# Graph attention over 32 graphs: TensorE turns every third head, the values of all groups run one graph later

## The reference

```python
q, k, v = (split_heads(x @ W + b) for W, b in ((Wq, bq), (Wk, bk), (Wv, bv)))
scores = einsum('bhqd,bhkd->bhqk', q, k) / sqrt(32) + beta * adj
scores = where(adj > 0, scores, -9e15)
out = einsum('bhqk,bhkd->bhqd', softmax(scores), v)     # heads joined again
y = layernorm(x + out)                                  # over the 384 features
```

## Time and profile before

| | |
|---|---|
| median of 3 runs | 704.23 us (703.93 to 704.75) |
| the profiled execution's own time | 703.96 us |
| its span, first to last instruction | 702.1 us |
| busy PE / DVE / ACT / POOL | 634.2 / 602.2 / 586.2 / 408.1 us |
| mean granted TensorE clock | 0.993 |
| share of the span: PE / PEld / DVE / ACT | 90% / 73% / 86% / 83% |

### The profile page before, as it was taken

The page is one execution under the profiler, slowest core; times in us unless marked ns, Lnnn a source line. Parts: engine busy times, 40 slices in busy tenths (PEclk is TensorE's granted clock), DMA queues, the critical chain, the costliest instruction groups (busy, mean ns, idle before and its releaser), DMA issues. The chain is left out here.

```text
span 702.1 us, 21340 instructions
## 1 busy us (share of the span) xinstructions
PE 634.2 (90%) x6304; PEld 514.6 (73%) x6304; DVE 602.2 (86%) x2385; ACT 586.2 (83%) x2024; POOL 408.1 (58%) x642
## 2 busy tenths in 40 slices
PE   5889999999999999999999999999999999999991
PEld 5777777777777787877787877777777777777760
DVE  3888898889898888889888989888989888989885
ACT  4798888888888889888888888888888888888891
POOL 3311466765566775556675556676556676555643
PEclk9999999999999999999999999999999999999997
DMA  7065555557655557655556755556765555765441
GB/s 247 2 159 121 135 152 139 140 139 181 171 139 153 144 122 180 174 148 151 143 123 171 181 150 152 143 126 157 181 159 144 151 137 137 181 159 127 119 104 68
DMA packets 68226, 101.93 MB, mean 145 GB/s; under 512 B 10512, under 2 KB 36368, under 8 KB 68112
## 3 DMA queue, kind: packets, MB, share of 16 engines
q1 hardware_dynamic: 67024, 100.37, 55.9%
q10 hardware_dynamic: 1088, 0.20, 0.1%
HBM read 22.94 MB, written 12.58 MB: 51 GB/s over the span
## 5 line engine op out<-in xcount | busy, mean ns | idle before, releaser
L433 ACT ACTIVATE probs<-neg_scores,neg_max 128x256 f32<-128x256 f32 x768 | 381.6, 502 | 4.6 <-DVE neg_max L515 3.1
L515 DVE CUSTOM_DVE_ANT_0 neg_scores<-s_bank,bias_sb 128x256 f32<-128x256 f32 x768 | 287.4, 414 | 62.4 <-ACT probs L433 30.8
L554 DVE STREAM_TRANSPOSE blocks<-probs 128x512 f32<-128x512 f32 x248 | 175.1, 706 | 0.0
L433 ACT ACTIVATION_READ_ACCUMULATOR probs<-neg_scores,neg_max 128x1 f32 x768 | 148.0, 193 | 0.0
L399 PE MATMUL s_bank<-qk 32*128 32x256 f32 x1536 | 110.0, 399 | 23.5 <-DVE neg_max L515 21.9
L399 PEld LDWEIGHTS s_bank<-qk 32*128 32x128 f32 x1536 | 71.2, 184 | 64.5 <-issue 48.2
L326 PE MATMUL j_bank<-xt_high,w_high 128*128 128x256 f32 x576 | 115.6, 309 | 2.0 <-ACT w_high L465 1.7
L750 POOL TENSOR_SCALAR o_sb<-y_sb,rstd,shift 128x384 f32<-128x384 f32 x60 | 98.9, 1654 | 9.6 <-POOL shift L745 9.6
L369 PE MATMUL j_bank<-ident,probs 128*128 128x128 f32 x544 | 84.2, 278 | 21.2 <-ACT xt_high L454 20.8
L326 PE MATMUL j_bank<-xt_high,w_low 128*128 128x256 f32 x576 | 99.5, 281 | 0.0
L326 PE MATMUL j_bank<-xt_low,w_high 128*128 128x256 f32 x576 | 99.5, 281 | 0.0
(11 more groups left out here) (56 smaller groups left out, 957.5 us busy)
## 6 DMA issues: line engine op xcount, KB each, us to landing
shuffled<-blocks SPq DMA_DIRECT2D x496, 128.0 KB, 2.4
x_sb<-in_x_dram SPq DMA_DIRECT2D x32, 384.0 KB, 3.3
out_dram<-o_sb SPq DMA_DIRECT2D x30, 384.0 KB, 4.3
adj_sb<-in_adj_dram SPq DMA_DIRECT2D x32, 256.0 KB, 3.8
out_dram<-o_sb SPq DMA_DIRECT2D x4, 192.0 KB, 2.1
blocks<-in_L_gnn_Wq_dram SPq DMA_DIRECT2D x1, 576.0 KB, 5.9
blocks<-in_L_gnn_Wk_dram SPq DMA_DIRECT2D x1, 576.0 KB, 8.8
blocks<-in_L_gnn_Wv_dram SPq DMA_DIRECT2D x1, 576.0 KB, 9.6
```

Of the source, the lines that this page charges most:

```text
L433: nc.scalar.activation(probs[:, (T * s + t) % (T * NX), :], neg_scores[:, (T * s + t) % (T * NH), :], ACT.Exp, bias=neg_max[:, n % 2, t, h ...
L515: nc.vector.tensor_tensor_reduce(neg_scores[:, (T * s + t) % (T * NH), :], s_bank[h % J][:, t * N:(t + 1) * N], bias_sb[:, n % 2, t, :], - ...
L554: nc.vector.transpose(blocks[:, n % 2, :, h, :, :].rearrange("p k t q -> p t k q"), probs[:, slot:slot + T, :].rearrange("p t (k q) -> p t ...
```

## The change

`by_blocks` becomes true for heads with h % 3 != 2: PE turns heads 2, 5, 8 and 11, DVE and the transfers the other eight. So each group has both kinds (3, 3 and 2 heads by DVE). O and G of group 2 move from graph n-1 to n-2 at the same steps. X of the first third moves from step 5 to step 1, K of group 1 from step 5 to 3, V of the first tile from step 3 to 5. The DVE program is put in another order within a step, with the statistics moved from step 8 to step 10 and the seed from 9 to 11. SP issues the adjacency load and the store before the load of x, and the store is that of graph n-3. POOL adds the residual after it has prepared that of the next graph. In the last graph, the copies of heads 0 to 7 go into `shuffled` (`place_of`).

```diff
     def by_blocks(n, h):
-        return n < B - 1 and h < HV
+        return n < B - 1 and h % 3 != 2
...
-                1: (("K", 0, n + 1),),
+                1: (("X", 0, n + 2), ("K", 0, n + 1)),
                 2: (("G", 1, n - 2), ("Q", 0, n + 1)),
-                3: (("V", 0, n + 1),),
-                4: (("O", 2, n - 1),),
-                5: (("X", 0, n + 2), ("K", 1, n + 1)),
-                6: (("G", 2, n - 1), ("Q", 1, n + 1)),
+                3: (("K", 1, n + 1),),
+                4: (("O", 2, n - 2),),
+                5: (("V", 0, n + 1),),
+                6: (("G", 2, n - 2), ("Q", 1, n + 1)),
...
-    last_jobs = (("G", 1, B - 1), ("O", 2, B - 1), ("G", 2, B - 1))
+    last_jobs = (("G", 2, B - 2), ("G", 1, B - 1), ("O", 2, B - 1), ("G", 2, B - 1))
...
+        def place_of(n, h):
+            if n == B - 1 and h < HV:
+                half = shuffled[:, n % 2, :, :, :, :, :].rearrange("p k a h t q -> p (k a h t q)")
+                return (half[:, h * T * N:(h + 1) * T * N].rearrange("p (k q) -> p k q", k=T), ("O", 2, n - 2))
+            i = J * n + (h // 3 if n < B - 1 else h - HV)
+            before = i - NP
+            return (probs_t[:, i % NP, :, :], ("O", (3 * (before % J) + 2) // J, before // J) if before >= 0 else None)
...
                 for k in range(T):
                     for j in range(J):
                         h = J * g + j
                         if by_blocks(n, h):
-                            probs_k = shuffled[:, n % 2, k, :, h, :, :]
+                            probs_k = shuffled[:, n % 2, k, :, h - h // 3, :, :]
                         else:
-                            probs_k = probs_t[:, turned_before[H * n + h] % NP, k, :]
+                            probs_k = place_of(n, h)[0][:, k, :]
...
-                    if h % J in (1, 2) and s + 3 < B * H:
-                        maxima(s + 3)
+                    if h % J == 1:
+                        for ahead in (s + 3, s + 4):
+                            if ahead < B * H:
+                                maxima(ahead)
+                        for job in jobs_of(n, h):
+                            take(job)
+                    elif h % J == 2:
+                        for job in jobs_of(n, h):
+                            if job[0] in "TG":
+                                take(job)
+                    if h % J in (2, 3) and s + 4 < B * H:
+                        maxima(s + 4)
                     if by_blocks(n, h):
                         turn_blocks(n, h)
-                    if h % J in (2, 3) and s + 4 < B * H:
-                        maxima(s + 4)
...
-                    if h == 8 and n >= 2:
+                    if h == 10 and n >= 2:
                         for t in range(T):
                             moments(n - 2, t)
                         gather_moments(n - 2)
-                    if h == 9 and n >= 2:
+                    if h == 11 and n >= 2:
                         seed(n - 2)
```

More of the change, by code:

```diff
@@ L76, in jobs_of @@
                 0: (("O", 1, n - 2),),
-                1: (("O", 2, n - 1),),
+                1: (("O", 2, n - 2),),
                 2: (("G", 1, n - 2),),
-                3: (("G", 2, n - 1),),
+                3: (("G", 2, n - 2),),
                 5: (("O", 0, n),),
@@ L84, in jobs_of @@
                 10: (("G", 0, n - 1), ("G", 1, n - 1)),
-                11: (("O", 1, n),),
+                11: (("O", 2, n - 1), ("O", 1, n)),
             }
@@ L234, in wait_job @@
             eng.wait_ge(job_ready, place[job] + 1)
-        def reader(i):
-            n, h = (i // J, HV + i % J) if i < J * (B - 1) else (B - 1, i - J * (B - 1))
-            return "O", h // J, n
+        def place_of(n, h):
[5 more added lines that the diff above has]
+            return (probs_t[:, i % NP, :, :], ("O", (3 * (before % J) + 2) // J, before // J) if before >= 0 else None)
         def wait_probs_free(eng, s):
@@ L270, in shuffle @@
                 if n >= 2:
-                    wait_job(sp, ("O", 1, n - 2))
+                    wait_job(sp, ("O", 2, n - 2))
                 for c in range(J):
@@ L292, in _ @@
                 shuffle(n)
+                if n + 3 < B:
+                    load_adj(n + 3)
+                if n >= 3:
+                    store(n - 3)
                 if n + 4 < B:
                     load_x(n + 4)
[L295 to L298, removed]
+            store(B - 4)
             store(B - 3)
@@ L338, in values @@
             def values(g, n, b):
-                if by_blocks(n, J * g):
+                if n < B - 1:
                     pe.wait_ge(shuffled_in[n % 2], (n // 2 + 1) * J * J * DMA)
-                else:
-                    wait_taken(pe, place["T", J * g + J - 1, n])
+                wait_taken(pe, max(place["T", h, n] for h in range(J * g, J * (g + 1)) if not by_blocks(n, h)))
                 wait(pe, taken_a, act_taken[place["V", T - 1, n] + 1])
@@ L348, in values @@
                         if by_blocks(n, h):
[L349 removed]
+                            probs_k = shuffled[:, n % 2, k, :, h - h // 3, :, :]
                         else:
[L351 removed]
+                            probs_k = place_of(n, h)[0][:, k, :]
+                            if n < B - 1:
+                                probs_k = probs_k.rearrange("p (t a q) -> p a t q", t=T, a=J)
                         mm = pe.matmul(b[HD * j:HD * (j + 1), 0:N], v_sb[:, n % 3, k, h * HD:(h + 1) * HD],
@@ L443, in take @@
                 if kind == "T":
[L444 to L447, removed]
+                    copy, left = place_of(n, a)
+                    if left:
+                        wait_job(act, left)
+                    ins = nc.scalar.activation(copy, b[:, :].rearrange("p (k q) -> p k q", k=T),
                                                ACT.Identity)
@@ L456, in take @@
                     heads, values = heads_t[:, heads_slot[a, n], :], b[:, 0:N]
-                    if by_blocks(n, J * a):
+                    if n < B - 1:
                         heads = heads.rearrange("p (t a q) -> p a t q", t=T, a=J)
@@ L526, in take @@
                     wait_job(dve, job)
[L527 to L530, removed]
+                    copy, left = place_of(n, a)
+                    if left:
+                        wait_job(dve, left)
+                    ins = nc.vector.tensor_copy(copy, b[:, :].rearrange("p (k q) -> p k q", k=T))
                 elif kind == "K":
@@ L553, in turn_blocks @@
                 slot = T * (H * n + h) % (T * NX)
-                nc.vector.transpose(blocks[:, n % 2, :, h, :, :].rearrange("p k t q -> p t k q"),
+                nc.vector.transpose(blocks[:, n % 2, :, h - h // 3, :, :].rearrange("p k t q -> p t k q"),
                                     probs[:, slot:slot + T, :].rearrange("p t (k q) -> p t k q", q=HD)).then_inc(blocks_ready, 1)
@@ L600, in norm_last @@
                     if i == 1:
-                        for job in last_jobs[1:]:
+                        for job in last_jobs[2:]:
                             take(job)
@@ L679, in _ @@
                         gather_moments(n - 2)
-                    if h == 9 and n >= 2:
+                    if h == 11 and n >= 2:
                         seed(n - 2)
-                    for job in jobs_of(n, h):
-                        take(job)
+                    if h % J != 1:
+                        for job in jobs_of(n, h):
+                            if h % J != 2 or job[0] not in "TG":
+                                take(job)
             invert(B - 1, G - 1)
-            take(last_jobs[0])
+            for job in last_jobs[:2]:
+                take(job)
             norm_last()
@@ L762, in _ @@
                 if n >= 2:
+                    add_residual(n - 2)
                     layer_norm(n - 2)
```

2 lines of the change are left out of this document (removed).

## The result

The changed kernel takes 752.06 us (median of 4 runs, 750.89 to 753.79) against 704.35 for the kernel before: 1.0679 of its time, 95% interval 1.0656 to 1.0703. I had predicted slower, 726.7 with a range of 713 to 741. The direction was right, the time lies 11 us above the range. Of the values (O and G), only those of group 2 stand one graph later than before; groups 0 and 1 keep their places, which the title puts too broadly.

What follows compares the result with a forecast made beforehand. The prediction took PE to set stretches A and B and DVE to set C, 21.65 us per graph against 20.90. The sum was 703.96 - 2.1 + 21.0 + 0.4 + 3.4 = 726.7 us, range 713 to 741.

Steps and rivals of the forecast that it cites:

- Against a rule: Two PE idles, 0.61 and 0.70, become one of 2.0 per graph; the sum nevertheless stands at the full clock level.
- Clock falls: Rival: a third of B runs at the lower clock level, 2.4 us more per graph, 790 us; chance 0.02.
- B: Stretch from step 4's to step 8's scores: PE sets it, its 0.70 wait goes, 7.40 to 7.35 us.
- A: Stretch from step 0's to step 4's scores: its 0.61 wait goes, 6.86 to 6.49 us.
- C: Stretch from step 8's scores to the next step 0: DVE sets it, PE idles 2.0, 6.64 to 7.81 us.
- The wait for X's bank: In A, PE's Q waits 0.20 us for the bank that DVE frees by taking X.
- The way in: The first two graphs, before the steady part: 37.5 us against 40.47, plus 0.9 start-up lateness, so -2.1.
- Shuffle late: Rival: the shuffle lands 2.0 us later, so PE waits 0.7 before O of group 0: +20, 746 us; chance 0.06.
- The way out: The last graphs: +0.4 us in all for graph 30 and +3.4 for the end, bounds 1.0 to 5.3.
- the last copy waits for the store of graph 29: Graph 31: that store lands at 701.4, the last copy into the same slot could begin by 698.1; 3.4 us in all.
- The copies' wait for O of group 2: Graph 31: copies of heads 0 and 1 wait for graph 29's O; ACT's chain loses about 0.8 us.
- Sum: Per graph 6.49 + 7.35 + 7.81 = 21.65 us against 20.90, +0.75; +21.0 over 28 graphs.

Runs made afterwards that it cites:

- experiment 1: Changed kernel plus 12 filler matmuls on PE in its wait ahead of the step-0 scores, graphs 2 to 29: 731.89 us, ratio 1.0396.
- experiment 3: Kernel before the change, with the statistics moved to step 10 and done twice there, second results unused: 792.88 us, ratio 1.1254.
- Experiments 4: Kernel before the change, with only the statistics moved to step 10 and the seed to step 11: 725.13 us, ratio 1.0295.
- experiment 5: Changed kernel with statistics back at step 8, seed at step 9, and POOL adding the residual first: 698.71 us, ratio 0.9922.
- experiment 7: Kernel of experiment 5, with DVE taking X and K between step 1's two maxima and step 10's block transpose first: 687.45 us, ratio 0.9762.
- experiment 9: Kernel of experiment 7, with O of group 2 of graph 29 run in the last graph's step 0, ahead of O of group 1: 686.38 us.

## Why the prediction was wrong

*The step that failed* is the one under *Against a rule*, and with it the rival *Clock falls*. I gave it 0.02 on the strength of the mean of 0.993, and that row bears on idles of 0.61 and 0.70 only. I had written myself that no row has an idle of 2.0; a mean over a kernel without the idle is no evidence on a kernel with it. The sum puts the clock at its full level, and so it prices the idle of 2.0, which it forecast rightly, by the wait alone; through the clock that idle cost 20 us more. The Trainium skill ("TensorE: Matmul & The Clock Gate", section "HAM oscillation") says that idle ahead of each burst makes the burst begin at the lower level again. The trace agrees in part: the clock fell in 17 of 28 graphs and not in each, and 0.2 to 1.6 us into the burst rather than at its beginning. That the idle is the cause, experiments 1 and 3 show from both sides. The rival was also put in the wrong place and at the wrong price: it is not B but A, the stretch right behind the idle, and not 2.4 us in each graph but about 1.35 in three of five. (Its own sum is off too: 726.7 and 28 x 2.4 make 793.9, not 790.) The cost is 752.06 - 731.89 = 20.2 us, enough to leave the range.

*C, bound by DVE*: right, and the reason too. Experiments 4 and 5 show it with that part alone and with all but it. The term was 7.81 and is 7.96: the statistics are 1.34, not 1.22. I had taken the aggregates of the earlier trace rows as 0.33, less than their 0.41 by the usual overlap; with maxima right behind them they cost 0.44.

*A and B*: 6.49 and 7.35 predicted; 6.43 to 6.51 and 7.26 measured where the clock holds. The wait for X's bank is there; experiment 7 took it away. A period without a fall is 21.65 or 21.73, as forecast, but with some luck: A and B are 0.06 and 0.09 under their terms, C is 0.15 over its own. The mean of experiment 1, with a few disturbed graphs, is 21.74.

*The way in*: predicted -2.1, measured -0.3. Two waits were missed, 0.8 in C of graph 0 (7.06, not 6.25: DVE's take of X waits 0.71 for ACT's xt_high) and 1.0 in B of graph 1 (8.18, not 7.21). The second is the rival *Shuffle late*, in that graph:

```profile
56.30 0.41 PE L360 MATMUL j_bank<-shuffled,v_sb 128*32 128x256 f32 x2 [1.08 <-DVE xt_low L544]
```

That shuffle's last transfer had landed at 56.10. In the steady part of the changed kernel the wait is nearly absent, as forecast, for C is long enough: graph 18 alone has it, 0.2 (B of 7.47), behind issues that took 12.97. When C shrank (experiments 5 and 7) the spare was gone, in some graphs.

*The way out*: predicted 0.4 and 3.4, measured 5.1. Of it 1.7 is graph 30 (22.27 against 20.54), nearly all of it the fall, since without one it took 20.79 in experiment 1. The last 3.3 are graph 31's, near the 3.4 predicted, but not for the reason given. I held that the last copy waits for the store of graph 29. It doesn't: POOL ends that graph at 745.29, its store landed at 747.81, 2.5 later and not 4.3, and the last copy starts at 747.95, 0.40 behind the one ahead of it as in the kernel before. It was close, 0.14. The copies' wait for O of group 2, which I had priced at 0.8, is 2.84 on DVE, and experiment 9 took 2.1 off that wait and 1.7 off the two last graphs. Size right by luck, cause wrong.

*Sum*: the kernel with the clock held is at 731.9, 5.2 above the forecast and inside the range. In its profiled execution (731.39, 4.7 above) the way in takes 2.6 more than predicted (B of graph 1 and C behind it are long there), the period 0.09 x 28 = 2.5, and the way out 0.2 less.

## What to carry to other kernels

Ask where in the loop through a shared set of banks a piece of work stands: the same 1.34 us of statistics is free between the last and the next first reader, and costs 33 us in this kernel two steps later with the clock held, 53 with the falls. When a change turns two short waits of TensorE into one long one, price the clock as well as the wait, and don't take a good mean clock without such a wait as proof. If the wait can't go, splitting it, or a few cheap matmuls in it, kept the clock up here.

## What the runs showed of the hardware that I had not expected

- The granted clock falls after one idle of 1.9 to 2.0 us per graph, though PE is busy for nearly all of the other 20. The number of falls grows with the length of the unbroken idle, in one profiled execution of each kernel: none at 0.60, 0.67 and 1.25, 1 in 27 at 1.48, 17 in 28 at 1.91, 21 in 28 at 2.03. Split in two (0.48 and 1.43) the same 1.91 brought none in the steady graphs.
- Which graph falls isn't settled: graph 3 and graph 4 look alike up to the fall in graph 4, 1.3 us after the idle. In experiment 3 two graphs fall and the third doesn't from graph 10 to 24, and from 25 on all six fall; the changed kernel is less regular. What the chip goes by there stays open.
- Each stretch at the lower level lasts 3.4 us, and its beginning is not tied to the end of the idle: 0.2 to 1.6 us after PE has resumed in the changed kernel, and in experiment 3 from 0.1 us before (0.4 in graph 26) to 1.7 us after.
- The 16 issues of a shuffle take 10.2 to 13.0 us in the changed kernel, with the same instructions, and 12.73 in the row of experiment 5. There most issues take 0.6 each, and two take 1.5 and 2.1. I haven't found what holds those up; it decides whether O of group 0 waits once C is short.
